# A graph layer with batch norm: late branch, tests inside the loop, x in pieces, 156 counted groups for 158

## The reference

```python
msg = node_feat[src] + edge_feat
neigh = jax.ops.segment_sum(msg, dst, num_segments=node_feat.shape[0])
rst = (1.0 + eps[0]) * node_feat + neigh
h = rst @ W1 + b1
mean = jnp.mean(h, axis=0)
var = jnp.var(h, axis=0)
h = (h - mean) * jax.lax.rsqrt(var + BN_EPS) * gamma + beta
h = jax.nn.relu(h)
out = h @ W2 + b2
...
x = _layernorm(x + out, axis=-1)
```

## Time and profile before

| | us |
|---|---|
| median of 3 runs (265.67 to 265.93) | 265.71 |
| the profiled execution | 265.49 |
| its span, first to last instruction | 263.7 |

### The profile page before, as it was taken

One profiled execution on the slowest core, in us unless ns is written; L12 is line 12 of the kernel. 1 busy time (PEld: TensorE's weight loads), 2 busy tenths in 40 slices (PEclk: granted clock), 3 DMA queues, 4 the chain that ended last, 5 costly groups with the idle time before them and its releaser, 6 DMA issues.

```text
span 263.7 us, 6841 instructions
## 1 busy us (share of the span) xinstructions
PE 240.7 (91%) x2205; PEld 201.5 (76%) x2205; DVE 187.8 (71%) x686; ACT 127.9 (48%) x225; POOL 172.6 (65%) x113
## 2 busy tenths in 40 slices
PE   0649689999999999999999999999999999999980
PEld 0548568889999998788888888878888879845980
DVE  2978894768789986887887878777666511288882
ACT  0406512445565665455645555544444232176794
POOL 3058888888888888888888888888888600270000
PEclk9999956999999999999999999999999999999996
DMA  5975655677789888777888787877776400000034
GB/s 156 271 232 109 138 115 100 151 153 177 192 193 209 189 196 193 171 184 189 200 186 187 183 193 176 192 165 176 156 160 155 81 0 2 4 0 0 2 114 130
DMA packets 48957, 38.11 MB, mean 145 GB/s; under 512 B 5019, under 2 KB 47947, under 8 KB 48921
## 3 DMA queue, kind: packets, MB, share of 16 engines
q1 hardware_dynamic: 32829, 30.62, 40.3%
q0 software_dynamic: 14400, 6.56, 20.8%
q10 hardware_dynamic: 1692, 0.48, 1.0%
HBM read 36.05 MB, written 1.60 MB: 143 GB/s over the span
## 4 chain that ended last, share of the span: by engine, by line
PE 79%; DVE 12%; issue 3%; ACT 2%; DVEq 2%; DMA 1%; ACTq 1%
PE ps L682 28%; PE ps L690 20%; PE ps L720 9%; PE ps L714 7%; PE ps L636 4%; PE ps L781 3%; PE ps L706 2%; DVE hit_k L952 2%; PE ps L770 2%; DVE hit_k L949 2%; DVE aggT L1022 2%; PE ps L711 1%; ACT big L561 1%; DMA x_room<-in_dst_dram 1%; PE ps L619 1%
## 5 line engine op out<-in xcount | busy, mean ns | idle before, releaser
L438 POOL DMA_INDIRECT egat<-in_x_dram,srci x100 | 163.6, 1636 | 43.1 <-issue 28.3
L524 ACT ACTIVATE big<-ps 128x500 f32 x158 | 96.7, 612 | 109.8 <-PE ps L720 83.6
L690 PEld LDWEIGHTS ps<-hit_c,ebuf 128*128 128x128 f32 x632 | 103.2, 195 | 14.9 <-DVE hit_c L920 4.7
L690 PE MATMUL ps<-hit_c,ebuf 128*128 128x20 f32 x632 | 97.3, 232 | 6.4 <-DVE hit_c L920 4.6
L1022 DVE TENSOR_TENSOR aggT<-aggT,ps 128x20 f32 x208 | 35.9, 173 | 54.9 <-PE ps L690 35.5
L682 PE MATMUL ps<-big,xN 128*128 128x114 f16 (+8 forms) x225 | 59.7, 278 | 0.4 <-ACT big L524 0.3
L682 PE MATMUL ps<-big,x_room 128*128 128x114 f16 (+8 forms) x225 | 59.6, 278 | 0.0
L682 PE MATMUL ps<-big,xr 128*128 128x114 f16 (+8 forms) x225 | 59.5, 278 | 0.0
L720 PE MATMUL ps<-hit_k,hit_l 128*128 128x400 f16 x158 | 53.2, 337 | 0.0
L714 PE MATMUL ps<-hit_k,hit_l 128*128 128x300 f16 x158 | 46.5, 294 | 0.0
L952 DVE TENSOR_TENSOR hit_k<-iota_k,key 128x800 f16<-128x800 f16 x79 | 44.9, 568 | 0.0
(11 more groups left out here) (105 smaller groups left out, 209.3 us busy)
## 6 DMA issues: line engine op xcount, KB each, us to landing
ebuf<-in_edge_attr_dram SPq DMA_DIRECT2D x79, 256.0 KB
egat<-in_edge_attr_dram SPq DMA_DIRECT2D x49, 128.0 KB
egat<-in_x_dram,srci POOLq DMA_INDIRECT x100
out_dram<-big SPq DMA_DIRECT2D x5, 256.0 KB
w_sb<-in_L_gnn_W_dram ACTq DMA_DIRECT2D x2, 128.0 KB, 6.9
out_dram<-big SPq DMA_DIRECT2D x2, 128.0 KB
x_room<-in_dst_dram SPq DMA_DIRECT2D x1, 192.0 KB
x_room<-in_src_dram ACTq DMA_DIRECT2D x1, 192.0 KB
```

The costliest lines, as they stand in the source:

```text
L438: return nc.gpsimd.indirect_dma_start(to, None, x[:, :], bass.IndirectOffsetOnAxis(ap=ix, axis=0), compute_op=op)
L524: nc.scalar.activation(cnt[:, :, bass.ds(lows[m % LOADS], WIN)], ps[:, m % BANKS_C, 0:KEYS].rearrange("p (t n) -> p t n", n=WIN), ACT.Copy ...
L690: last = nc.tensor.matmul(ps[:, SUMS + w % BANKS_S, 0:WIN], rows_v[:, j * D:(j + 1) * D], hits_v, start=(j == 0), stop=(j == ROWS - 1))
```

## The change

- The flag is no longer awaited before the loop. All engines run the fast path's loop at once; the tests are computed inside it, at windows 86 and 89 on DVE, joined over partitions by a PE product at window 92, and stored as the flag at window 95. The branch comes after the loop: on DVE before the last block's addition, on ACT before the hidden layer is stored, on PE between the preloads 4 and 5, on POOL and SP where they have nothing more to do. The general path then starts anew, with its lists and x loaded again.
- So that wrong lists can do no harm meanwhile, the first rows are clamped to within MARGIN - 1 = 29 of nominal (two operations on DVE, in `firsts`).
- The lists lie at the end of `big`, which is now cleared at window 89, and not in the room of `x3`.
- Prologue: ACT copies `rel`, `srci` and `carry` out of the turns instead of DVE; the key copies on DVE come right behind the keys; `hits_c(0)` and the clamps stand ahead of `hits_k(0)`. The weight transfers go from ACT's queue to SP's, behind the first slots.
- x comes in seven pieces, in turns with chunks and slots, each with its semaphore.
- 156 groups are counted and 52 gathered. Blocks are (10, 12, 17, 25, 31, 31, 20, 10) groups with 120, 180, 256, 376, 468, 466, 302 and 218 columns; MARGIN is 30 for 36.
- The second half's keys begin at offset 5 (WIN_B = 15): 375 columns at line 720; DVE's row has 376 per group.

```diff
-FROM_B = 4
-WIN_B = WIN - FROM_B
-GROUPS_C = 158
-BLOCKS_C = (10, 12, 17, 25, 31, 31, 22, 8, 2)
+FROM_B = 5
+WIN_B = 15
+GROUPS_C = 156
+BLOCKS_C = (10, 12, 17, 25, 31, 31, 20, 10)
...
-MARGIN = 36
+MARGIN = 30
...
+        TEST_F = 3
+        W_BOUNDS = READY[TEST_F] + 2
+        W_TESTS = W_BOUNDS + 3
+        W_WORST = W_TESTS + 3
+        W_SHARED = W_WORST + 3
...
         @block.sync
-            sp.dma_start(xN[:, 0:NT - 1, :], x_main).then_inc(x_loaded, 16)
-            sp.wait_ge(x_padded, 1)
-            sp.dma_start(xN[0:NL, NT - 1, :], x[(NT - 1) * P:N, :]).then_inc(x_loaded, 16)
+            def x_piece(b):
+                t0, t1 = pieces(b)
+                if b < NB - 1:
+                    sp.dma_start(xN[:, t0:t1, :], x_main[:, t0:t1, :]).then_inc(x_loaded[b], 16)
...
-            for n in range(SLOTS):
-                slot(n)
-                if n < CHUNKS:
-                    chunk(n)
-            sp.wait_ge(path_known, 1)
+            chunk(0)
+            x_piece(X_ORDER[0])
+            slot(0)
+            x_piece(X_ORDER[1])
+            chunk(1)
+            x_piece(X_ORDER[2])
+            slot(1)
+            x_piece(X_ORDER[3])
+            chunk(2)
+            x_piece(X_ORDER[4])
+            slot(2)
+            x_piece(X_ORDER[5])
+            chunk(3)
+            x_piece(X_ORDER[6])
+            for n in range(3, SLOTS):
+                slot(n)
+            sp.dma_start(w1_sb[:, :], w1).then_inc(weights_loaded, 16)
...
         @block.scalar
             nc.scalar.activation(srcf, srcq, ACT.Copy).then_inc(src_rows_made, 1)
+            act.wait_ge(rel_turned, 1)
+            nc.scalar.activation(spread(rel[:, :]), banked(2), ACT.Copy).then_inc(rel_made, 1)
             act.wait_ge(lo_turned, 1)
...
+            act.wait_ge(src_turned, 1)
+            nc.scalar.activation(spread(srci[:, :]), banked(7)[:, QC:Q, :], ACT.Copy).then_inc(sources_made, 1)
+            act.wait_ge(carry_turned, 1)
+            nc.scalar.activation(carry[:, :].rearrange("p (q h) -> p q h", h=2),
+                                 ps[:, 1, 0:GC].rearrange("p (h q) -> p q h", q=QC), ACT.Copy).then_inc(carry_made, 1)
...
         @block.tensor
+                if w == W_WORST:
+                    pe.wait_ge(worst_found, 2)
+                    pe.wait_ge(block_added, TEST_F)
+                    nc.tensor.matmul(ps[:, ACC + (TEST_F + 1) % 2, 0:1], ones[0:Q, :], over[:, TESTS + 1:TESTS + 2],
+                                     start=True, stop=True).then_inc(worst_shared, 1)
...
+            pe.wait_ge(x_b2_added, 1)
+            preload(0, 4)
             pe.wait_ge(path_known, 1)
             flag = pe.value_load(wide[0:1, 0:1], min_val=0, max_val=1)
+            with pe.If(flag == 0):
+                pe.wait_ge(hidden_stored, NB * HH)
+                preload(4, len(ROW_PIECES))
+                products()
...
         @block.vector
+            dve.wait_ge(constants_made, 8)
+            dve.wait_ge(rel_made, 1)
+            hits_c(0)
+            dve.wait_ge(firsts_loaded, 32)
+            dve.wait_ge(constants_made, 10)
+            nc.vector.tensor_tensor(firsts[:, :], firsts[:, :], least_first[:, 0:G], ALU.max).then_inc(lows_made, 1)
+            dve.wait_ge(lows_made, 1)
+            nc.vector.tensor_tensor(firsts[:, :], firsts[:, :], most_first[:, 0:G], ALU.min).then_inc(lows_made, 1)
+            nc.vector.tensor_tensor(rel[:, T - ROWS:T], rel[:, T - ROWS:T], pads[:, :], ALU.add).then_inc(rel_made, 1)
+            dve.wait_ge(key_made, 1)
+            dve.wait_ge(lo_made, 1)
+            hits_k(0)
...
+                if w == W_BOUNDS:
+                    find_bounds()
+                if w == W_TESTS:
+                    find_worst()
...
+                    nc.vector.memset(cnt[:, :, CNT - SPARE:CNT], 0.0).then_inc(spare_zeroed, 1)
+                if w == W_SHARED:
+                    dve.wait_ge(worst_shared, 1)
+                    nc.vector.tensor_scalar(wide[:, :], ps[:, ACC + (TEST_F + 1) % 2, 0:1], 0.5, None,
+                                            ALU.is_gt).then_inc(wide_made, 1)
...
+            dve.wait_ge(path_known, 1)
             flag = dve.value_load(wide[0:1, 0:1], min_val=0, max_val=1)
+            with dve.If(flag == 0):
+                last_sums()
+                hidden_stats(hidden_stored)
+            with dve.Else():
...
```

More of the change, by code:

```diff
@@ L243, in gnn_layer @@
         firsts_loaded = sem("firsts_loaded")
-        x_loaded = sem("x_loaded")
+        x_loaded = [sem(f"x_loaded{b}") for b in range(NB)]
         x_padded = sem("x_padded")
@@ L344, in gnn_layer @@
         X_TILES = [(i, t) for i, b in enumerate(X_ORDER) for t in range(*pieces(b))]
+        TEST_F = 3
[3 more added lines that the diff above has]
+        W_SHARED = W_WORST + 3
+        assert W_SHARED + 2 < READY[TEST_F + 1] and sum(w in C_OF for w in range(W_SHARED)) < CORNER
         @block.sync
@@ L621, in turn_x, with hidden @@
                         last.then_inc(x_turned, 1)
+            def hidden(n0, n1, complete, made, stored):
+                for n in range(n0, n1):
+                    b, h = n // HH, n % HH
+                    pe.wait_ge(complete, b + 1)
+                    if n >= BANKS_C:
+                        pe.wait_ge(stored, n - BANKS_C + 1)
+                    nc.tensor.matmul(ps[:, n % BANKS_C, 0:width(b)], w1_sb[:, h * P:(h + 1) * P],
+                                     aggT[:, b * BANK:b * BANK + width(b)], start=True,
+                                     stop=True).then_inc(made, 1)
@@ new lines, in _, with preload @@
+            multiply(F - 1, 0, UNITS)
+            pe.wait_ge(counts_stored, GC)
+            pe.wait_ge(weights_loaded, 80)
+            hidden(0, NB * HH, sums_complete, hidden_made, hidden_stored)
+            def preload(a0, a1):
+                for a in range(a0, a1):
+                    t0, t1 = ROW_PIECES[a]
+                    r = rows_of(t1 - 1)
+                    nc.tensor.matmul(ps[0:r, (a + 4) % 8, 0:(t1 - t0) * D], ident[0:r, 0:r],
+                                     xN[0:r, t0:t1, :].rearrange("p t d -> p (t d)"), start=True, stop=False,
+                                     skip_group_check=True)
@@ new lines, in products @@
+            def products():
+                for a, (t0, t1) in enumerate(ROW_PIECES):
+                    b = t0 // 4
+                    pe.wait_ge(relu_half0_made, b + 1 + max(0, b + 1 - ACT_FROM))
+                    pe.wait_ge(relu_half1_made, min(b + 1, ACT_FROM))
+                    for t in range(t0, t1):
+                        r = rows_of(t)
+                        k = (t - t0) * P
+                        for h in range(HH):
+                            last = nc.tensor.matmul(ps[0:r, (a + 4) % 8, k:k + D], hT[:, h, t * P:t * P + r], w2_sb[:, h, :],
+                                                    start=False, stop=(h == HH - 1), skip_group_check=True)
+                    last.then_inc(rows_made, 1)
@@ L785, in _ @@
+                hidden(0, NB * HH, gen_sums_complete, gen_hidden_made, gen_hidden_stored)
+                pe.wait_ge(gen_hidden_stored, NB * HH)
+                preload(0, len(ROW_PIECES))
+                products()
         @block.vector
@@ L876, in _ @@
-            dve.wait_ge(key_turned, 1)
-            key_d = key[:, :, :].rearrange("p (q k) two -> p q k two", k=HJ)
-            for a in range(2):
-                last = nc.vector.tensor_copy(key_d[:, :, :, a], banked(3)[:, 0:QC, :])
-            last.then_inc(slots_made, 1)
-            dve.wait_ge(carry_turned, 1)
-            nc.vector.tensor_copy(carry[:, :].rearrange("p (q h) -> p q h", h=2),
-                                  ps[:, 5, 0:GC].rearrange("p (h q) -> p q h", q=QC)).then_inc(slots_made, 1)
```

796 lines of the change are left out of this document (410 added, 386 removed).

## The result

| | before | after |
|---|---|---|
| median, us (6 runs each) | 265.69 (265.31 to 265.93) | 267.73 (266.92 to 269.04) |
| ratio, 95% interval | | 1.0083 [1.0051, 1.0115] |
| profiled execution, us (its span) | 265.49 (263.7) | 269.04 (267.1) |

The change makes the kernel 2.0 us slower; 4.0 us faster was forecast, and 266.0 was the upper end. The time after lies outside the range, on the side to which 0.13 was given, and the prediction's own sign of being wrong came: a second stretch of 0.50 near 100 us. Its runs spread over 2 us where those of before spread over 0.6.

The account below looks back on a forecast made before the run. Lists and DVE were taken to bound the start, DVE the early loop, PE's columns the rest from 44 us. Terms -3.3 - 0.2 - 3.6 + 3.0 + 0.1 = -4.0 us gave 261.7 against the median, range 259.2 to 266.0.

Parts of the forecast that it names:

- the side to which 0.13 was given: Whole kernel: the change makes it slower than before, chance 0.13.
- the prediction's own sign of being wrong: A second stretch of granted clock 0.50 near 100 us, or first products waiting for x or the list.
- (3): PE from window 14 on: fewer columns at 0.43 ns each, fewer groups and smaller blocks gain 3.6 us.
- (4): Tests inside the loop, windows 86 to 95: DVE bursts stall PE, a loss of 3.0 us, bounds 1.5 and 4.0.
- (1): Prologue: less DVE work ahead of `hits_k(0)`, which starts at 11.5 to 12.1; gain 3.3 us, bounds 1.0 and 4.2.
- The rival of a late list: Prologue: the list of first rows lands late between SP's transfers, gain only 1.0, 264.0 us; chance 0.10.
- (2): Windows 0 to 13, paced by DVE: one-hot rows of 752 for 800 elements save 0.2 us over seven pairs.
- What the sum left to a rival: The clock falls to 0.50 in the tests' stall, +4.3 us, 266.0 in all; chance 0.22.
- (5): After the loop: branches mostly covered by PE's last block and preload; cost 0.1 us, bounds 0 and 1.5.
- the early stretch at the lower level doesn't come back: PE early in the loop stays at 2.4 GHz, -2.5 us, 259.2 in all; chance 0.13.
- The gathers did set the pace: Rival at the loop's last gather: 2.4 us to spare, used up if POOL starts at 13.8; 262.7 us, chance 0.05.

Follow-up runs that it names:

- the probe: The changed kernel with six extra products in each of 32 counted groups, in eight row forms; spacings of 147.9 to 179.2 ns, no total time given.
- its variant: The kernel before with only the second half's counts in rows of 14 from offset 6, 350 columns for 400; 262.67 us, ratio 0.9846.
- the changed kernel's second profile: The changed kernel run once more, unaltered, beside other variants; ratio 1.0105, profiled execution 264.27 us.

## Why the prediction was wrong

The steps that failed are three: the columns (3), whose price was carried over to a form in which it doesn't hold; the tests (4), whose fall of the clock was left out of the sum; and the early transfers in (1), which were taken to move as before.

**(1) Prologue: DVE's work right, the early transfers wrong, 1.3 us.** -2.0 for -3.3; `hits_k(0)` at 12.9 to 13.9 in all the profiles of changed kernels, not 11.5 to 12.1. From DVE's first operation on `dst` on the gain is 3.4 us, as forecast, though the parts differ a little (the clamps 0.36 each for 0.3, two waits for PE of 0.44 and 0.45 for 0.3). What failed is "as long as the early transfers move as before" and "small transfers do no harm if they are queued": `dst` landed 1.4 us later, 1.0 to 2.0 us in the eleven profiles with pieces and 0.3 in the one profile with x in one transfer. So the order of the transfers behind `dst` on SP's queue costs most of it; which of them holds `dst` up isn't shown. The rival of a late list named the wrong list: with pieces nothing waited for the first rows, and in the one profile in which `dst` was early they were waited for, 0.50 us. The first gather came at 12.5, 0.96 us behind the copy of its indices, not at 10.4.

**(2)** The rows of 752 take DVE 541 ns for 568, 27 ns less where 34 were the most: 0.2 us over seven pairs, as forecast. Whether it is felt can't be told, since the first windows go by the history of the clock, below.

**(3) Columns: the step that failed in its mechanism.** "0.43 ns a column" came from two forms, 300 and 400 columns, with rows of 12 and 16, both even and at even offsets; it was carried over to rows of 15 from 5. By windows 124 to 193 the term of -1.7 us is 156 x 10 ns = +1.6: 3.3 us of error (the probe's 179.2 - 168.5 = 10.7 gives 3.4, the 6 ns of the other profiles 2.6). The rest of the step held: the last block took 7.01 us, and windows 193 to the hidden layer gained 0.6.

**(4) Tests: place and stalls right, the fall of the clock missing from the sum.** The collision with both register loads was where it was said to be (the small operations are twelve, not fourteen). (4) had stalls of 1.5 and 2.8 us, 4.3 in all. PE waited 1.86 and 1.12 us in the first profile, the second at the lower level. In the variant with 400 columns, where the level held until 113.39 us, it met both at 1.00, and they were 1.89 and 2.38 us, 4.3:

```profile
108.00 0.40 PE L739 MATMUL ps<-hit_c,ebuf 128*128 128x20 f32 x2 [1.89 <-DVE aggT L1100]
...
113.42 0.62 PE L739 MATMUL ps<-hit_c,ebuf 128*128 128x20 f32 x2 [2.38 <-DVE aggT L1100]
```

What the sum left to a rival came with it in each of the seven profiles in which these tests stand as the change put them and nothing fills PE: a stretch of 0.50 that begins between 104.8 and 113.4 us, 3.4 to 13.7 us long. In five of them it begins 0.6 to 1.6 us behind the first wait, in one (rows of 14) in the last 0.2 us of it, and in both cases ahead of the second. That first wait is 1.81 to 1.86 us long, so the fall doesn't take the two stalls together that the rival counted. Of the seven in which the tests are absent, in small steps or covered by fillers, or which are the kernel before and its variant, none has it; their longest wait there is 1.39 us. The rival's price was 4.3 us; without tests PE is busy 4.2 less. It was given 0.22 and should have been the case. In the median the whole of the tests is worth 3.0 to 3.5 us (without them, in small steps), so there the fall isn't told apart from the stalls.

**(5) The end: a term not foreseen.** The branches cost nothing that a trace shows. But one of the last output transfers, the sixth or the seventh, is issued in 0.86 to 1.25 us, in all twelve profiles of changed kernels (with 400 columns the fourth too, 1.02), where the sixth and seventh took 0.37 and 0.45 before. It stands ahead of the last ones: 0.4 to 0.7 us between ACT's last operation and the end. Why that issue is long was not tried.

**The rivals.** That the early stretch at the lower level doesn't come back held in the first profile (-3.4 us from `hits_k(0)` to window 30) but belongs to the execution, not to the change: the changed kernel's second profile had two such falls. The gathers did set the pace, but not at the end: early, where the loop is ahead, three profiles wait 0.6 to 1.2 us at window 73. In windows 50 to 80 PE used gathered rows some 13 us behind the end of their instruction before, and 3.6 to 5 after.

Summed for the profiled execution, with 10 ns for the form: 3.3 (form) + 1.3 (prologue) + 3.7 (tests, 6.7 for 3.0) + 1.2 (gathers) + 0.6 (end, for 0.1) - 2.6 (early stretch: 3.4 for the 0.8 that (2) and (3) put into these windows) = 7.5, and the forecast missed it by 269.04 - 261.5 = 7.5. The terms are read off this one execution; that they add up checks the sum, not each term. In the second profile, 2.8 us above the forecast, the tests' stretch is 0.7 over its forecast and the gathers cost nothing. The median's 6.0 lies between; how often each history comes isn't known, so the median isn't split further.

## What to carry to other kernels

A price per column holds for the form from which it was taken. Before columns are trimmed, look whether the rows written still begin and end on an even one; here rows of 16 cost as much as rows of 15 from an even offset and less than those from an odd one, and 14 from an even offset was 12% cheaper. Work that is taken off the prologue and put into a loop needs a place without another burst: the same tests cost 3.5 us less in steps of at most 0.7 us than in two blocks beside register loads. A stall on PE in mid-kernel has to be priced twice, once as waiting and once as the lower level after it; here one wait of 1.8 us was enough for the second price. And transfers that are moved up in a queue are to be weighed against the list that everything waits for, which landed 1.0 to 2.0 us later here.

## What was unexpected of the hardware

TensorE's level has a history that differs between executions of one kernel. The rise to 2.4 GHz came at 18.4 to 31.9 us in eleven profiles (the one with products ahead of the loop aside), and at 44.8 and 47.8 us in two, with PE busy 13.30 of the 13.30 us before one of these:

```profile
44.80:57.00 12.20, 12.20 (x149) 10.86 (x148) 7.43 (x28) 4.92 (x9) 10.37 (x7) 1.00 0.72 156
31.40:44.70 13.30, 13.30 (x78) 11.32 (x78) 7.45 (x26) 3.67 (x6) 10.96 (x8) 1.00 0.59 124
```

(the granted clock has no record before the rise, and the view shows 1.00; the 78 products in 13.3 us against 149 in the 12.2 behind the rise tell the level). Where it came at 31 to 32, no fall followed before 60 us and window 20 started at 42.8 to 43.3; where it came at 18 to 26, a fall of 3.4 to 10.2 us followed at 26 to 35, and window 20 started at 42.8 to 47.9. The Trainium skill ("TensorE: Matmul & The Clock Gate", section What's actually happening) puts the variation of that instant at half a microsecond either way; these profiles spread over 13 us and more, and the two of the same code lie 12 us apart (31.4 and 19.4). So one profiled execution of such a kernel can be 5 us off another of the same code (269.04 and 264.27; the kernel before itself took 263.4 to 270.1 us in the later series), and a difference is to be read from stretches whose clock is the same in both.
